# Fewer semaphore tests on TensorE in the expert blocks of a graph attention and mixture-of-experts kernel, with other work moved beside them

## The reference, cut to what matters

```python
logits = xf @ gate_w + gate_b
probs = jax.nn.softmax(logits, axis=-1)
top2_vals, top2_idx = jax.lax.top_k(probs, 2)
cw = jnp.zeros((N, Ee)).at[jnp.arange(N)[:, None], top2_idx].add(top2_vals)
def step(acc, params):
    w1, bb1, w2, bb2, we = params
    h = jax.nn.gelu(xf @ w1 + bb1, approximate=False)
    y = h @ w2 + bb2
    return (acc + we[:, None] * y, None)
out, _ = jax.lax.scan(step, jnp.zeros_like(xf), (W1, b1, W2, b2, cw.T))
x = x + out      # x before: (8, 1024, 128); D 128, H 256, E 8; xf is layernorm(x)
```

## Time and profile before

| | us |
|---|---|
| median of 3 runs | 891.76 |
| lowest, highest | 889.36, 894.33 |
| the profiled execution's own time | 890.94 |
| its span in the profile | 889.1 |
| expert blocks: first L1654 to last L1654 on PE | 691.5 to 877.4 |
| PE busy in 700 to 860 us of the span | 159.92 of 160 |
| DVE, ACT, POOL busy there | 130.75, 109.39, 76.02 |

### The profile page before, as it was taken

How to read it: one execution, slowest core, us unless ns; L and a number is a source line. 1 busy time by engine, 2 the same in 40 slices (tenths; PEclk the granted TensorE clock), 3 DMA queues, 4 the chain that set the end, 5 groups by cost and what they waited for, 6 DMA issues and landing times.

```text
span 889.1 us, 21028 instructions
## 1 busy us (share of the span) xinstructions
PE 733.5 (83%) x6443; PEld 374.3 (42%) x6443; DVE 754.1 (85%) x2135; ACT 582.7 (66%) x1136; POOL 556.6 (63%) x564
## 2 busy tenths in 40 slices
PE   4379689999999999999999997656411999999995
PEld 2222222322323223223233234635301888888884
DVE  4569999999999999999999999885741788888883
ACT  4377577796897887877968775534200766666662
POOL 0204556786886877877869879677773344444443
PEclk9679989999999999999999998555555999999998
DMA  8952200403204005004032003001111122222210
GB/s 286 263 82 74 70 1 26 118 2 87 58 1 132 12 24 120 2 27 117 1 92 53 2 1 96 1 32 37 52 53 46 51 56 68 66 67 66 53 51 2
DMA packets 46449, 54.41 MB, mean 61 GB/s; under 512 B 7540, under 2 KB 29137, under 8 KB 46338
## 3 DMA queue, kind: packets, MB, share of 16 engines
q10 hardware_dynamic: 13824, 25.17, 10.8%
q1 hardware_dynamic: 27554, 19.31, 8.5%
q0 software_dynamic: 4960, 8.58, 3.0%
HBM read 34.03 MB, written 20.75 MB: 62 GB/s over the span
## 4 chain that ended last, share of the span: by engine, by line
DVE 35%; PE 33%; issue 13%; POOL 12%; DMA 3%; ACT 3%; SPq 1%; ACTq 1%; POOLq 0%; DVEq 0%
DVE rspread L938 8%; DVE prob_ring L917 7%; DVE w L917 5%; DVE prob_ring L928 5%; PE sum_ps L1656 4%; POOL rows_dram L529 4%; PE score_ps L1421 3%; PE sum_ps L1435 2%; PE score_ps L1381 2%; PE side_ps L1448 2%; PE score_ps L1382 2%; PE score_ps L1383 2%; POOL ctx_sb L469 2%; PE sum_ps L1662 2%; PE sum_ps L1660 2%
## 5 line engine op out<-in xcount | busy, mean ns | idle before, releaser
L1421 PE MATMUL score_ps<-stack_mem 128*128 128x512 f16 x512 | 158.5, 392 | 44.1 <-DVE prob_ring L917 31.3
L469 POOL TENSOR_TENSOR ctx_sb<-ctx_sb,rspread 128x512 f32<-128x512 f32 x108 | 138.7, 1284 | 57.8 <-DVE rspread L938 48.9
L690 ACT ACTIVATE prob_ring<-prob_ring 128x1024 f32<-128x1024 f32 x128 | 134.4, 1055 | 60.4 <-DVE prob_ring L917 48.8
L690 ACT ACTIVATE w<-w 128x1024 f32<-128x1024 f32 x128 | 134.2, 1056 | 49.0 <-DVE w L917 48.9
L917 DVE SCALAR_TENSOR_TENSOR w<-score_ps,limit 128x1024 f32<-128x1024 f32 x128 | 152.8, 1213 | 15.5 <-PE score_ps L1421 15.4
L536 POOL DMA_INDIRECT out_x<-xn,limit x91 | 89.7, 986 | 115.1 <-DVE xn L1283 110.3
L917 DVE SCALAR_TENSOR_TENSOR prob_ring<-score_ps,limit 128x1024 f32<-128x1024 f32 x128 | 152.7, 1197 | 0.5 <-PE score_ps L1421 0.4
L474 POOL TENSOR_TENSOR ctx_acc<-ctx_acc,ctx_sb 128x512 f32<-128x512 f32 x93 | 119.3, 1283 | 7.3
L1421 PEld LDWEIGHTS score_ps<-stack_mem 128*128 128x128 f16 x512 | 29.5, 98 | 210.5 <-DVE prob_ring L917 109.3
L812 ACT ACTIVATE xn<-score_ps,vec 128x128 f32<-128x128 f32 x364 | 104.2, 369 | 14.6 <-PE score_ps L1383 14.6
L938 DVE STREAM_SHUFFLE rspread<-prob_ring 128x256 f32<-128x256 f32 x256 | 101.7, 449 | 0.0
(11 more groups left out here) (221 smaller groups left out, 1505.9 us busy)
## 6 DMA issues: line engine op xcount, KB each, us to landing
stack_mem<-qk_dram ACTq DMA_DIRECT2D x64, 256.0 KB, 4.8
ctx_sb<-rows_dram SPq DMA_DIRECT2D x91, 66.5 KB, 1.9
qk_dram<-qk_hi ACTq DMA_DIRECT2D x16, 256.0 KB, 2.9
qk_dram<-qk_lo ACTq DMA_DIRECT2D x16, 256.0 KB, 4.1
x<-in_adj SPq DMA_DIRECT2D x4, 512.0 KB, 7.5
ctx_sb<-in_adj SPq DMA_DIRECT2D x4, 512.0 KB, 9.9
w<-in_L_ffn_W SPq DMA_DIRECT2D x4, 512.0 KB
rows_dram<-gather SPq DMA_DIRECT2D x29, 66.5 KB, 8.8
```

What stands on the lines that cost most here:

```text
L469: pool.tensor_tensor(fresh, fresh, by, ALU.mult).then_inc(scaled_ready, 1)
L690: act.activation(prob_at(s, u), prob_at(s, u), ACT.Exp, scale=1.0 / SCORE).then_inc(exp_done, 1)
L1421: ins = pe.matmul(score_ps[:, h, :], kstack[:, par, h, k * P:k * P + P], qstack[:, par, h, half * HALF:half * HALF + HALF], start=True, st ...
```

## The change

What it does, engine by engine:

- PE: of the eleven tests of semaphores a block, two are left. Both stand inside `second(i)`: before L1660 (now L1679) a test that both gelus of block i+1 are done (`ready_for_hidden(i + 3)`), and before L1662 (now L1682) a test that the low half of block i+3 is done (`ready_for_turn(i + 4)`). All others are implied by what DVE and ACT do in order. Before the loop `turn_blk(3)` now stands behind tests for both gelus of block 0, for three low halves and for six weight copies.
- DVE: `blk_norm` also waits for the bias rows. The weight copies of block i+4 are made in round i, one block earlier than before, and the load of the registers stands after `blk_low`. The address of the store is no longer computed here.
- POOL: `aim(i)` computes the address with one TENSOR_SCALAR (a maximum with `barred`) before `store(i)`, when the block's rows are loaded and the store eight blocks back has landed. `store(i)` tests its result.
- SP: eight registers are loaded for four blocks in one instruction, in place of two for each.

The diff, cut to its core:

```diff
             for i in range(BLOCKS):
-                sp.load(block_at, row_table[0:1, 2 * i:2 * i + 2])
-                first = sp.snap(block_at[0], min_val=0, max_val=DUMMY)
-                pair_at = sp.snap(block_at[1], min_val=0, max_val=E * E - 1)
+                if i % 4 == 0:
+                    load_places(i // 4)
+                first = sp.snap(places[i // 4 % 2][2 * (i % 4)], min_val=0, max_val=DUMMY)
+                pair_at = sp.snap(places[i // 4 % 2][2 * (i % 4) + 1], min_val=0, max_val=E * E - 1)
...
+            def aim(i):
+
+                pool.wait_ge(blk_loaded[i % AHEAD], 16 * (i // AHEAD + 1))
+                wait(pool, stored[i % AHEAD], 16 * (i // AHEAD))
+                if i == 0:
+                    pool.wait_ge(table_ready, 3)
+                pool.tensor_scalar(target[:, i % AHEAD:i % AHEAD + 1], blk[:, i % AHEAD, TOKEN:TOKEN + 1], barred[:, i:i + 1],
+                                   None, ALU.max).then_inc(target_ready, 1)
+
             def store(i):
 
+                pool.wait_ge(target_ready, i + 1)
                 pool.wait_ge(rows_ready, i + 1)
-                pool.wait_ge(target_ready, i + 1)
...
             for i in range(BLOCKS):
+                aim(i)
                 store(i)
...
                 dve.wait_ge(blk_loaded[i % AHEAD], 16 * (i // AHEAD + 1))
+                dve.wait_ge(b2_loaded[i % AHEAD], 16 * (i // AHEAD + 1))
                 wait(dve, blk_turned, i - AHEAD + 1)
...
                 row = blk[:, i % AHEAD, :]
-                dve.wait_ge(blk_loaded[i % AHEAD], 16 * (i // AHEAD + 1))
                 wait(dve, stored[i % AHEAD], 16 * (i // AHEAD))
-                dve.scalar_tensor_tensor(out=target[:, i % AHEAD:i % AHEAD + 1], in0=row[:, TOKEN:TOKEN + 1],
-                                         scalar=float(CAP - 1), in1=barred[:, i:i + 1], op0=ALU.min,
-                                         op1=ALU.max).then_inc(target_ready, 1)
                 dve.wait_ge(y_done, 2 * i + 2)
...
-            w1_copy(2, 0)
-            w1_copy(2, 1)
+            for i in range(2, 4):
+                w1_copy(i, 0)
+                w1_copy(i, 1)
             for i in range(BLOCKS):
                 if i + 4 < BLOCKS:
                     blk_norm(i + 4)
                 if i + 3 < BLOCKS:
-                    if (i + 3) % 4 == 0:
-                        load_experts((i + 3) // 4)
                     blk_low(i + 3)
-                    w1_copy(i + 3, 0)
-                    w1_copy(i + 3, 1)
+                if i + 4 < BLOCKS:
+                    if i % 4 == 0:
+                        load_experts(i // 4 + 1)
+                    w1_copy(i + 4, 0)
+                    w1_copy(i + 4, 1)
                 combine(i)
...
+            def ready_for_hidden(i):
+
+                if i - 2 < BLOCKS:
+                    pe.wait_ge(gelu_done, 2 * i - 2)
+
+            def ready_for_turn(i):
+
+                if i - 1 < BLOCKS:
+                    pe.wait_ge(blk_lo_ready, i)
+                elif i - 3 < BLOCKS:
+                    pe.wait_ge(rows_ready, i - 4)
...
-                wait(pe, rows_ready, i - 1)
-                pe.wait_ge(b2_loaded[i % AHEAD], 16 * (i // AHEAD + 1))
                 pe.matmul(sum_ps[:, i % 2, 0:2 * P], unscale[:], b2_ring[:, i % AHEAD, :], start=True, stop=False)
-                pe.wait_ge(gelu_done, 2 * i + 1)
                 pe.matmul(out_of(0), hid[:, i % 4, 0, 0, :], w2_at(0, at), start=False, stop=False)
                 at_1 = weights_at(i, 1)
                 pe.matmul(out_of(0), hid[:, i % 4, 0, 1, :], w2_at(1, at), start=False, stop=False).then_inc(y_done, 1)
-                pe.wait_ge(gelu_done, 2 * i + 2)
+                ready_for_hidden(i + 3)
                 pe.matmul(out_of(1), hid[:, i % 4, 1, 0, :], w2_at(0, at_1), start=False, stop=False)
                 following = next_at()
+                ready_for_turn(i + 4)
                 pe.matmul(out_of(1), hid[:, i % 4, 1, 1, :], w2_at(1, at_1), start=False, stop=True).then_inc(y_done, 1)
...
             for i in range(3):
+                pe.wait_ge(blk_normed, i + 1)
+                wait(pe, blk_lo_ready, i - 1)
                 turn_blk(i)
             for i in range(2):
-                hidden(i, 0)
-                hidden(i, 1)
+                pe.wait_ge(blk_lo_ready, i + 1)
+                for e in range(2):
+                    pe.wait_ge(w1_copied, 2 * i + e + 1)
+                    hidden(i, e)
+            ready_for_hidden(2)
+            ready_for_turn(3)
+            pe.wait_ge(w1_copied, 2 * 3)
```

More of the change, by code:

```diff
@@ L400, in _, with load_places @@
             sp.wait_ge(chunk_added, STEPS * NB)
-            block_at = [sp.alloc_register(name) for name in ("row_at", "pair_at")]
+            places = [[sp.alloc_register(f"place_{j}_{n}") for n in range(8)] for j in range(2)]
+            def load_places(c):
+                last = min(4 * c + 4, BLOCKS)
+                sp.load(places[c % 2][0:2 * (last - 4 * c)], row_table[0:1, 8 * c:2 * last])
             for i in range(BLOCKS):
-                sp.load(block_at, row_table[0:1, 2 * i:2 * i + 2])
-                first = sp.snap(block_at[0], min_val=0, max_val=DUMMY)
-                pair_at = sp.snap(block_at[1], min_val=0, max_val=E * E - 1)
+                if i % 4 == 0:
+                    load_places(i // 4)
+                first = sp.snap(places[i // 4 % 2][2 * (i % 4)], min_val=0, max_val=DUMMY)
+                pair_at = sp.snap(places[i // 4 % 2][2 * (i % 4) + 1], min_val=0, max_val=E * E - 1)
                 if i >= AHEAD:
@@ L1615, in turn_blk @@
             def turn_blk(i):
-                pe.wait_ge(blk_normed, i + 1)
-                wait(pe, blk_lo_ready, i - 1)
                 turn(side(i % 2)[:, 0:P], blk_x2[:, i % AHEAD, :], ident[:]).then_inc(blk_turned, 1)
@@ L1630, in hidden @@
                 u = 2 * i + e
-                if e == 0:
-                    pe.wait_ge(blk_lo_ready, i + 1)
-                pe.wait_ge(w1_copied, u + 1)
-                wait(pe, gelu_done, u - 3)
                 for k in range(KH):
```

## The result

| | us |
|---|---|
| changed kernel, median of 4 runs (lowest, highest) | 905.08 (904.22, 906.58) |
| kernel before beside it, median of 4 runs | 891.23 (889.36, 894.33) |
| ratio, 95% interval | 1.0154 (1.0121 to 1.0186) |
| profiled execution after: its time, its span | 906.58, 904.8 |
| first and last store of an expert block | 694.64, 896.00 (before 694.52, 880.34) |

The changed kernel is 1.5% slower. The forecast was 892.0 with a range of 889.5 to 904.0: wrong in its value, and the measured time lies 1 us above the range. Rival A (901 to 906) is what happened.

The account below looks back on a forecast made before the run. PE was taken to bound the kernel at 2.078 us a block, with POOL just under at 2.04. PE 1.1 us earlier (0.6 + 0.5), then POOL's tail, ended 0.5 later: 891.4, named as 892.0, range 889.5 to 904.

Parts of the forecast that it names:

- Rival A: POOL's store loop: its cycle of 2.18 to 2.24 us exceeds PE's 2.078, giving 901 to 906 us; chance 0.37.
- the pauses: PE beside the bias product: 0.09 + 0.21 = 0.30 us a block, from changing between 2 and 128 rows, not tests.
- PE's tests worth 0: PE's sequencer: nine tests fewer, 0.46 us a block, all beside array work, so 0 on the path.
- Cost 0: PE's new test before the last product, for the low half three blocks ahead: some 0.4 us remain, so no cost.
- POOL's cycle of 2.04: POOL's loop per block: 0.79 + 0.97 + 0.08 + 0.20 = 2.04 us, just under PE's 2.078.
- after a few blocks: Within rival A: the ring of eight and SP's test of target_ready soon make other engines follow POOL's beat.
- The start, 0.6 us won: First blocks: three SP loads fewer make PE's second product begin earlier, worth 0.6 us, bounds up to 1.8.
- Copies 0.5: DVE's weight copies one block ahead: some 0.5 us won from late copies, between 0 and 0.6.
- The tail, 0.5 later: Last blocks: POOL cannot follow stores 1.3 us apart, so the last store comes at 880.8, 0.5 us later.
- row of 1.11 us: Profile row of a DMA_INDIRECT behind tensor work taking 1.11 us, not 0.97; it would make POOL's cycle 2.18.

Follow-up runs that it names:

- e6: Kernel before with the bias product's weights padded from 2 to 128 rows with zeros, all eleven tests kept: 885.76 us, ratio 0.9861.
- e2: Changed kernel with the token column (the store's address) back on DVE, all else as changed: 889.98 us, ratio 0.9990 to the kernel before.
- e3: Kernel before with one edit, SP loading its registers for four blocks at once: 889.49 us, ratio 0.9984.
- e7: Changed kernel with the token column back on DVE and the bias product's weights padded to 128 rows: 879.31 us, ratio 0.9792 to the kernel before.
- e9: As e7, with the token column made for four blocks by one DVE operation: ratio 0.9810 to the kernel before.
- e10: Kernel before with the bias product's weights padded to 128 rows and SP's loads for four blocks, nothing else of the change: 876.01 us, ratio 0.9754.
- e11: As e10, with DVE's copies one block further ahead and PE's tests as before: 896.52 us, ratio 0.9961 to the kernel before.
- e4: Changed kernel with POOL making the token column three blocks ahead of the store: 890.39 us, ratio 0.9995 to the kernel before.
- e5: Changed kernel with a second TENSOR_SCALAR, with a constant, on POOL in each block: ratio 1.0360 to the kernel before.
- e1: Kernel before with one edit, the token column moved from DVE to POOL: 906.79 us, ratio 1.0174.
- e8: Changed kernel with the token column three blocks ahead on POOL and the bias product's weights padded to 128 rows: 881.52 us, ratio 0.9808 to the kernel before.

## Why the prediction was wrong, point by point

- **What bounds the kernel, and the pauses: right.** PE's beat of 2.078 with 0.30 us of pauses beside the bias product stayed to the hundredth, and e6 shows that they go with the 2 rows. They are 0.10 us ahead of the product and 0.20 behind it. The Trainium skill (TensorEngine Tiling (Array Packing), Key Properties) says that a change of the tiling mode drains TensorE. Whether a product with 2 rows is such a change no record shows; e6 shows that this kernel pays for the change of rows and not for tests.
- **PE's tests worth 0: right** at 2.078 (e2 against e3, 183.57 and 183.75 us from block 1's bias product to the last). "Cost 0" for the new test before the last product was right at that beat only, as it closes a loop through DVE: the widened kernels have 1.82 with it (e7, e9) and 1.78 without (e10, e11). Of the 0.4 us that remained (0.39 in e4), 0.13 are the way from DVE to PE.
- **POOL's cycle of 2.04: the step that failed.** The sum had the right terms and two wrong sizes: TENSOR_SCALAR 0.20, measured 0.297 (0.24 by itself, the rest with the column as operand, e5); DMA_INDIRECT 0.97, measured 1.044, and 1.03 or more in every block; the gap 0.08 was 0.05, the 0.79 was 0.79. 2.18, not 2.04. So the store waited for POOL's own cycle and not for PE's beat. The text weighed 0.97 against 1.11 and argued that one small operation would leave the store at 0.97; e1, e4, e5 and e8 all have 1.04, e2, e3, e6, e9 and e10 0.97. A margin of 0.04 under PE's beat was trusted to terms of which two were known to 0.1. And the cycle was taken as constant: its mean is 0.05 above its median, 4.4 of the 15.5 us.
- **The other engines fall into POOL's beat "after a few blocks": wrong in the number.** It took 33 blocks. With a mean cycle the end is the same.
- **The start, 0.6 us won: not seen in this profile.** Block 0's bias product came at 690.60, near the forecast 690.1, but block 1's 0.45 us later than before. Counted from block 0's transposition it was 0.2 us earlier, and the clock rose 1.2 us later. Over 12 runs SP's loads for four blocks gave 1.4 us (e3), inside the bounds given (up to 1.8).
- **Copies 0.5: not shown as a price of the copies.** 0.49 us went in e4 and 0.24 in e2, which has the same copies.
- **The tail, 0.5 later: wrong.** In the changed kernel the last store comes 9.43 us behind the last bias product against 2.94 before, since POOL is blocks behind by then. Where POOL keeps up (e4, the same operations in another order) it is 3.07.
- **The range** ended at 904 since its upper end was to take in "most of A". A's own span, 901 to 906, was right, with the measured 905.1 in its upper half; its chance of 0.37 was too low beside a row of 1.11 us of just this kind. Its 2.18 us has luck in it: a DMA_INDIRECT taken too long (1.11 for 1.044) and a gap too long (0.08 for 0.05) made up for a TENSOR_SCALAR taken too short (0.20 for 0.297).

## What to carry to other kernels

A step moved to an engine that "has time" joins the loop of that engine: write down the loop (prepare, run, gap, new step), with the dearest row of each kind, and compare it with the beat; if it lies within a few per cent, make the step one that nothing waits for next, as e4 does, before anything else. In these runs the preparation of an indirect DMA on GpSimd (0.76 us) starts only when its test is met, so the wait for a thing just computed on the same engine puts its whole length on the path. A test moved on one engine can close a loop through another that shows only when the beat gets shorter: add up that loop too (e7, e8). And pauses beside a matmul with few rows are bought back with zeros: padding 2 rows to 128 gave more (1.4%, and 2.5% with SP's loads) than all that was taken off the sequencers.

## What the runs showed of the hardware

- DMA_INDIRECT on POOL takes 0.97 us behind another or behind idle time, and 1.04 behind a TENSOR_SCALAR of 0.3 us.
- A TENSOR_SCALAR of 128x1 on POOL takes 0.24 with a constant (e5) and 0.28 to 0.30 with a column as operand (e5, the changed kernel), and mostly 0.35 in e8, where the store's preparation runs beside it.
- Of the eight TENSOR_SCALARs of 0.39 to 0.59 in the changed kernel seven run beside a weight copy of DVE (L1287), and so do all 16 stores over 1.08; 56 other stores run beside a copy and aren't longer. No run isolates it.
- In the kernel before, the changed one and e1 to e5, two stores some 100 us behind the first lie 3.7 to 4.0 us apart (3.68 at 794.5 before, 3.78 at 801.6 after); in the kernel before and in the changed one the sequencer's 0.55 is 2.15 there. A POOL with slack hides it; where POOL is the bound it costs 1.6 us. Its cause isn't known.
- PE's clock rose from 1.2 to 2.4 GHz at moments over 5 us apart, counted from the same transposition (6.0 us in e2, 11.8 in the changed kernel), and 2 us apart in two kernels with the same PE program (10.6 before, 8.4 in e1).
